# Earlier mask loads, no common start barrier, and the later attentions' head outputs moved from VectorE to ScalarE, in a four-layer kernel with a new written-out order

## What is computed

```python
scores = jnp.einsum('bhqd,bhkd->bhqk', q, k) / jnp.sqrt(jnp.float32(HD))
scores = scores * mask - 10000.0 * (1.0 - mask)      # layer 2
probs = jax.nn.softmax(scores, axis=-1)
return jnp.einsum('bhqk,bhkd->bhqd', probs, v)
```

## Time and profile before

| | |
|---|---|
| runs | 1038.15, 1041.89, 1042.33 us |
| profiled execution, its own time | 1040.13 us |
| its span (first to last instruction) | 1038.2 us |
| mean granted TensorE clock | 0.979 of full speed |
| busy: PE / weight loads | 954.2 / 760.8 us |
| busy: DVE / ACT / POOL | 745.7 / 587.8 / 540.6 us |
| HBM read and written | 26.85 and 2.10 MB |

### The profile page before, as it was taken

The page is one execution under the profiler, slowest core; times in us unless marked ns, Lnnn a source line. Parts: engine busy times, 40 slices in busy tenths (PEclk is TensorE's granted clock), DMA queues, the critical chain, the costliest instruction groups (busy, mean ns, idle before and its releaser), DMA issues.

```text
span 1038.2 us, 27531 instructions
## 1 busy us (share of the span) xinstructions
PE 954.2 (92%) x10944; PEld 760.8 (73%) x10944; DVE 745.7 (72%) x1607; ACT 587.8 (57%) x1334; POOL 540.6 (52%) x666
## 2 busy tenths in 40 slices
PE   6868999898799999999999999999998879999996
PEld 4657877676478787778778777777775758887885
DVE  1378358878889979844765578779589979876764
ACT  2379753235355556578867672546653347655772
POOL 1365355535568856433465474256565655765331
PEclk9979999999899999999999999999999989999999
DMA  9601200100000110100011100000010000000001
GB/s 351 248 3 33 55 1 1 29 1 1 1 1 3 33 33 1 55 22 1 20 34 29 33 2 25 5 22 3 2 29 13 2 2 2 13 2 14 13 2 42
DMA packets 27501, 30.70 MB, mean 30 GB/s; under 512 B 14640, under 2 KB 24176, under 8 KB 26736
## 3 DMA queue, kind: packets, MB, share of 16 engines
q1 hardware_dynamic: 26352, 27.11, 8.0%
q10 hardware_dynamic: 1024, 1.85, 0.5%
HBM read 26.85 MB, written 2.10 MB: 28 GB/s over the span
## 4 chain that ended last, share of the span: by engine, by line
PE 53%; DVE 20%; DVEq 9%; issue 6%; POOL 5%; ACT 4%; POOLq 1%; DMA 1%; ACTq 0%
PE bank L494 7%; PE bank L506 7%; PE bank L399 7%; PE bank L378 6%; PE bank L366 6%; PE bank L391 4%; DVE lane L1007 3%; DVEq L1010 3%; DVE bank L1003 2%; PE bank L457 2%; PE bank L481 2%; PE bank L535 2%; DVEq L1004 2%; PE bank L524 2%; DVEq L863 2%
## 5 line engine op out<-in xcount | busy, mean ns | idle before, releaser
L1413 POOL TENSOR_TENSOR lane<-lane 128x512 f32<-128x512 f32 x160 | 167.3, 1052 | 183.4 <-DVE lane L884 103.6
L1180 ACT COPY lane<-bank 128x512 f32<-128x512 f32 x232 | 132.2, 592 | 149.2 <-PE bank L366 83.7
L366 PE MATMUL bank<-ident,lane 128*128 128x128 f32 x896 | 133.3, 283 | 20.2 <-POOL lane L1413 4.8
L366 PEld LDWEIGHTS bank<-ident,lane 128*128 128x128 f32 x896 | 103.2, 144 | 49.3 <-issue 22.2
L1482 POOL TENSOR_TENSOR lane<-lane 128x512 f32<-128x512 f32 x64 | 81.3, 1271 | 74.1 <-DVE lane L1007 73.4
L1007 DVE TENSOR_TENSOR_SCAN lane<-lane,bank 128x256 f32<-128x256 f32 x128 | 81.0, 674 | 5.0 <-issue 0.4
L882 DVE TENSOR_REDUCE lane<-lane 128x8 f32<-128x512 f32 x96 | 64.8, 675 | 18.0 <-ACT lane L1199 16.8
L1162 ACT ACTIVATE lane<-bank,vecs 128x256 f32<-128x256 f32 x112 | 55.6, 554 | 39.0 <-PE bank L366 38.8
L1199 ACT ACTIVATE lane<-lane 128x512 f32<-128x512 f32 x96 | 60.7, 636 | 23.0 <-DVE lane L864 22.6
L1148 ACT ACTIVATE lane<-lane 128x256 f32<-128x256 f32 x96 | 52.4, 595 | 28.9 <-POOL lane L1398 28.7
L494 PE MATMUL bank<-lane,w_d 128*128 128x256 f32 x256 | 60.8, 387 | 2.6 <-ACT lane L1162 1.1
(11 more groups left out here) (162 smaller groups left out, 2233.3 us busy)
## 6 DMA issues: line engine op xcount, KB each, us to landing
lane<-in_inT SPq DMA_DIRECT2D x16, 256.0 KB, 4.6
lane<-in_x SPq DMA_DIRECT2D x16, 256.0 KB, 2.8
w_d<-in_w_d SPq DMA_DIRECT2D x1, 3072.0 KB, 21.2
w_am<-in_w_am SPq DMA_DIRECT2D x1, 2048.0 KB, 15.1
lane<-in_inT SPq DMA_DIRECT2D x16, 128.0 KB, 3.0
lane<-in_ctx SPq DMA_DIRECT2D x8, 256.0 KB, 2.9
out_x<-lane SPq DMA_DIRECT2D x8, 256.0 KB, 2.2
w_c<-in_w_c SPq DMA_DIRECT2D x1, 1792.0 KB, 12.0
```

The source lines that it names most:

```text
L366: ins = pe.transpose(t[:, i * P:(i + 1) * P], src, ident[:, :])
L1180: s.copy(out, src).then_inc(bk.free_sem(key), 1)
L1413: p.tensor_tensor(q, q, den.unsqueeze(2).to_broadcast([P, n, 512 // n]), ALU.mult).then_inc(sig["normal"].sem, 1)
```

## The change

1. `mask0` is loaded by one DMA that copies the row to all 128 partitions, without a wait for `ready`; POOL's memset of `mask0_raw` goes. SP's order has `w_am`, then the four masks, then `w_b`, `w_c`, `w_d` in a row.
2. `ready` is split. DVE, ACT wait only for DVE's small constants and POOL's memsets; the gate's tanh and `self_c` move into the first `s_b` and `v_b` of lane 0, with waits where they are used in the first round. POOL doesn't wait. PE waits for `vecs` and `ident` only before lane 0's (and each lane's) first transposition.
3. The heads of self-, cross- and layer-3 attention are taken by ACT (`s_heads`): the first pair after the copy of the third `probsT`, the second pair at the end. Layer 0's stay on DVE.
4. `ORDER` and `BANKS` are new throughout. DVE now has 737 steps, ACT 721.

```diff
-    ("in_loaded", 2, 16), ("mask0_loaded", 4, 16), ...
+    ("in_loaded", 2, 16), ("mask0_loaded", 1, 16), ...
 ORDER = {
     "PE": (
-        "P0111110000222223333031211010120011021221021101021011002203021012321130210111332111112330100000000001233130211"
...
+        "P0000022021112212133333001020201012122010110100120100112213120122000120120200000200211202101332021130311113312"
...
     "DVE": (
-        "P0110223030101100112222211001100221112211101100110002001220102221302230322330332331123233130033113013131000001"
...
+        "P0020001002212232230010011221120121001100010011001112110221012220312231322313222000300333311333330330102233112"
...
     "ACT": (
-        "P0111100022223333010122111001010220112211210101010012002210202312203321110233013321300103312033032113011110000"
...
+        "P0000220210112123233300001220112211001201001100110102112201212320213200012012221012021033033233331331000331320"
...
     "SP": (
-        "0123PP0123PP110022331023001122000011110222213323333301232013"
+        "0123P0123PPP002211330123002211330000111122202133332301230123"
...
-        ready = Signal("ready", 3)
+        ready = Signal("ready", 4)
...
             def probsT(u):
+                if g < NL and u == 0:
+                    pe.wait_ge(load["vecs"].sem, load["vecs"].at(0))
...
         def _(pe):
-            pe.wait_ge(load["vecs"].sem, load["vecs"].at(0))
...
                 if tag == "self":
+                    if g < NL:
+                        v.wait_ge(load["consts"].sem, load["consts"].at(0))
...
-            for c in range(2):
-                for i in range(2):
-                    v_heads(v, g, tag, c, i, A.headsT[:, c, i::2, :], VALUE_BIAS[tag])
-                yield
...
+            if g == 0:
+                v.wait_ge(load["consts"].sem, load["consts"].at(0))
+                v.tensor_scalar(self_c[:, :], self_m[:, :], 10000.0, -10000.0, ALU.mult, ALU.add).then_inc(ready.sem, 1)
...
         def _(v):
             v.wait_ge(load["vecs"].sem, load["vecs"].at(0))
-            v.wait_ge(load["consts"].sem, load["consts"].at(0))
...
-            v.wait_ge(ready.sem, ready.at(0))
+            v.wait_ge(ready.sem, ready.at(0, 2))
...
+        def s_heads(s, g, tag, A, c):
+
+            for h in range(2):
+                key = (g, tag, "heads", c, h)
+                s.wait_ge(bk.full_sem(key), bk.full_at(key))
+                src = bk.tile(key)[:, 0:2 * S].rearrange("p (b q) -> p b q", q=S)
+                bias = VALUE_BIAS[tag]
+                s.activation(A.headsT[:, c, h::2, :], src, ACT.Identity, bias=vec(bias, c) if bias else 0.0).then_inc(bk.free_sem(key), 1)
+
         def s_attention(s, g, tag, A):
...
+                if step == PT_:
+                    s_heads(s, g, tag, A, 0)
+                    yield
...
+            s_heads(s, g, tag, A, 1)
+            yield
...
+            if g == 0:
+                s.wait_ge(load["consts"].sem, load["consts"].at(0))
+                s.activation(tgate[:, 1:2], tgate[:, 0:1], ACT.Tanh).then_inc(ready.sem, 1)
...
-            s.wait_ge(load["consts"].sem, load["consts"].at(0))
-            s.activation(tgate[:, 1:2], tgate[:, 0:1], ACT.Tanh).then_inc(ready.sem, 1)
-            s.wait_ge(ready.sem, ready.at(0))
+            s.wait_ge(ready.sem, ready.at(0, 2))
...
         def p_a(p, g):
-            p.wait_ge(bk.full_sem((g, "l0", "q", 0)), bk.full_at((g, "l0", "q", 0)))
+            if g >= NL:
+                p.wait_ge(bk.full_sem((g, "l0", "q", 0)), bk.full_at((g, "l0", "q", 0)))
...
-            for lane_ in lanes:
-                p.memset(lane_.mask0_raw, 0)
             p.drain().then_inc(ready.sem, 1)
-            p.wait_ge(ready.sem, ready.at(0))
...
                 if g < NL:
                     sp_in(sp, g)
                     yield
-                    sp.wait_ge(ready.sem, ready.at(0))
...
-                for j in range(4):
-                    sp.dma_start(L.mask0_raw[32 * j:32 * j + 1, :], a["mask0"][g]).then_inc(sig["mask0_loaded"].sem, 16)
+                sp.dma_start(L.mask0_raw, a["mask0"][g].partition_broadcast(P)).then_inc(sig["mask0_loaded"].sem, 16)
```

More of the change, by code:

```diff
@@ new lines @@
+        "23222321000032133012303003021121100012122202302031101120222303333330001211332303000101213121000201203032102003"
+        "33203302022311033330202220002330131003131203020230202321223020303232101021301313103211132000122120312323330321"
+        "32131132212301231322220212211113111111211132113300031031000013200203231133311130301333211110000211200310333022"
+        "12003131131102021122102113013010103021321211111331111131223003333210000102221331011222012132102132103230003110"
+        "30320033200322320302220223223230101032133302303233123133013322120012032122202111300222301031121333230231030032"
@@ new lines @@
+        "30000001312200002213020101101012222201201112100213003210210000000012103212330220033230000000000203333300322122"
+        "30333012223212222322333112123211111132112210223222222123113323033333133113132111111031123310000300133133333203"
+        "33313100113213011010000110020212122200001000210023110011113111011012110211113313331313232222211223232100211223"
+        "21022122132233003321331210033211013330033300003303300032230310210110202110122331120312222220102332220011020030"
+        "30003002013332111101001113313011200200030000003303112310302313311213211111311222122232132222033233333133332022"
@@ L108 @@
-        "02033030302000313030323330330303213223322031321133133300300103030113012313333111131112112123020000120021113232"
-        "11332211332022231322111323212131233333221332222311132210200230322233332230032232230013233133223221313322003112"
-        "2030333113333"
+        "P0000220210112123233300001220112211001201001100110102112201212320213200012012221012021033233033331331000331320"
+        "23021131121222302312030330000001330000001200013010023032033220031003200222000011002002322102202202123231232132"
@@ new lines @@
+        "11131311213210322112210301023220332331333213211011311232322123100010013311111332133133000311031000121032230320"
+        "11113333111001002121102010022002103011212211310033121101122110213013300103321331211123332232123331122032210122"
+        "20121231321330332003002330332332232333203233323201022003213212001130101310103323003003000011001010111110202100"
+        "00100100312021000202033212313013132112332211102212233202331002233120332111313123232222303220200210013213120013"
+        "3332233222332031323233231323233320113221122131132213333223333"
@@ L117 @@
-        "323323223333300333301122212013333"
+        "P0213000212203012121010010112102203123122003003113303020230110000113220000221123210101222120101132120032200010"
+        "01030322030330000300223330031221303303002222223312121121131213222221213312333311332112113123120300133111330333"
+        "30033331100110021120020210111110120123133132211223300121211212310301321030120013030003030002231311012023223112"
+        "02022221213322200030300330013311010110233110020300001330310100022331111131232122212233233313123212312223222323"
@@ L118 @@
+        "200033232333233203333112212133233"
     ),
     "SP": (
-        "0123PP0123PP110022331023001122000011110222213323333301232013"
+        "0123P0123PPP002211330123002211330000111122202133332301230123"
     ),
@@ L123 @@
 BANKS = (
[L124 to L133, removed]
+    "01234567012345670156720156726720672063742741201756562436503641051735710603064253064257235721305721305273015273"
+    "01523651204516702467520745207631452076315240152764370654274207657462513704625174307564163451062475124741547152"
+    "03202043271450361402735614730256147306214730562014627513634621727253467102505025052341026317250356372154637632"
+    "67321657312644042650427504327150643042304760237146054602504623237235713575137042651370261431740532174063521062"
+    "35610235461023546102361025367431604371607431024375103725140737532713524726407104326735672310540754602754306271"
+    "53406271563042715304271427574251732540173254016712673152675263475261043170453104210574631740263401567532427635"
+    "46203754176235167243014623462734061234506210261034726510347367235417026351635177027026473047230547631266126361"
+    "36205620542051473262056140404703570605716403572160435276104352437542367157054702547023754602160232607236723564"
+    "17203564107235641064712067342540640275346012701205327324057364126570314657203143026154370216543617524306751274"
+    "253170542316705416"
 )
@@ L1120, in v_d @@
             v.wait_ge(bk.full_sem(key), bk.full_at(key))
+            if g < NL:
+                v.wait_ge(ready.sem, ready.at(0))
             v.scalar_tensor_tensor(flat(x[:, :, :]), bk.tile(key)[:, :], tgate[:, 1:2], flat(x[:, :, :]), ALU.mult, ALU.add).then_inc(bk.free_sem(key), 1)
@@ L1422, in p_attention @@
                     if tag == "self":
+                        if g < NL:
+                            p.wait_ge(ready.sem, ready.at(0))
                         q = grid(A.probs[step])
```

27 lines of the change are left out of this document (4 added, 23 removed).

## The result

The changed kernel takes 1052.36 us (median of 4, 1045.27 to 1057.89), the kernel before 1041.16 us in the same series. The ratio is 1.0116 [1.008, 1.0152]: slower by 1.2%, where 1.1% faster was forecast, and above the range of 1013 to 1047. The four times follow the granted clock: 1045.27 us at a mean of 0.980, 1057.89 at 0.967.

The account below looks back on a forecast made before the run. PE was taken to bound the kernel, busy 954.2 of 1038.2 us. The terms -1.2 - 6.3 - 6 + 2 + 1 gave -10.5 us on 1040.13, so 1030 us was predicted, range 1013 to 1047.

Parts of the forecast that it names:

- What bounds the kernel: Whole kernel: PE bounds it, busy 954.2 of 1038.2 us; the change is worth what it does to 84 idle us.
- the prediction's last sentence: Forecast is wrong if PE's busy sum is unchanged and its idle time from 130 to 1010 us exceeds 51 us.
- Start of PE: Kernel start: PE begins at 6.8 us instead of 8.32, and 2.4 us of waiting for loads is dropped.
- the masks: Before lane 0's first scores: PE stalls 3.0 us on the mask; start and masks together gain 1.2 us.
- Scores among the projections: From 43 to 90 us: four units of exponentials done earlier take 6.3 us off PE's 16.1 us of idle time.
- Heads: Attention heads moved from DVE to ACT: 6 us gained in DVE-dense stretches, 2 and 1 us charged back.
- The new strings: New engine orders, with each round's 32 scan steps contiguous on DVE: charged 0, bounds -8 (gain) to +16 us.
- Rival B: Where four lanes scan together, scans crowd DVE and PE idles more: slower, 1046 to 1062 us; chance 0.15.
- Rival A: The start's gain is given back later, waiting for DVE in scan stretches: no change, 1037 to 1041 us; chance 0.2.
- Rival C: At the start the mask holds PE, stall 7.5 us or no gain there: still faster, 1034 or 1037; chance 0.15.

Follow-up runs that it names:

- old_order_both_edits: All edits of the change (early masks, split barrier, later heads on ScalarE) under the orders of the kernel before: 1034.49 us, ratio 0.9964.

## Why the prediction was wrong

*What bounds the kernel* was right, and the prediction's last sentence named the case that came: PE's idle time from 130 to 1010 rose to 60.4 us, over the 51 set as the mark, with PE's busy sum up by 0.6% only.

*Start of PE, the masks* had the right times, in part by luck. The first matmul came at 6.96 for 6.8, the mask at 20.0 for 20.5, the scores at 21.91 inside 21 to 22. But the stall of 3.0 us in front of them wasn't there: PE could have begun them at 21.8 at the earliest, not at 18.9. Its first seven steps took 14.9 us instead of 12.0, because the matmuls of the first `q` and `k0` started at half pace until 12.5 us. The 2.4 us that I read as waiting for loads in the kernel before, and dropped, were the same thing: there too the first matmuls stand 427 ns apart, without a gap. Two errors of 3 us cancelled.

*Scores among the projections* held under the new order. 43 to 90 gained 6.1 of the 6.3 us, and PE's idle time to 130 us fell by 7.5, as much as both terms together. The clock that PE kept there, another 3.7 us, wasn't in the sum. Taking the early masks and barriers away again cost 7 us. Under the old order a like move, with lanes 0 and 1, gave nothing.

*Heads* was right in mechanism. I took 3 net; the old order gave 1.7, the new one 15, within the bounds but five times the term. DVE's total came to 719 for 715, ACT's to 593 for 604, with 45 table loads for 48.

*The new strings* is the step that failed: "I charge 0, bounds -8 (gain) to +16". With the same edits the new strings cost 16 us, where the edits together are worth 4 in the old order. The 16 are even net of the early scores, which the forecast counts as a term of its own though they are part of the strings. By the two traces the strings give back some 10 us before 130 and lose 24.2 behind it, in idle time (11.9) and in clock (12.3), which the sum has nowhere. So the term that I set to nothing because it couldn't be read was the largest of all, and by itself it lies beyond its bound of 16.

The sum then reads: edits under the old order -0.36%, strings +1.53%, together +1.16%. The edits rescue part of what the order loses: without the heads on ScalarE the new strings cost 1.0262 / 0.9992, 28 us; with them 16. That is why edits that are worth 7 and 15 us under the new order don't add up to a gain over the kernel before.

*Rival B* had the sign and the place (stretches dense with scans), not the mechanism. It decides, I wrote, once PE idles over 10.5 us more there: the dense stretches idle 39.2 for 36.4, and with 44 us of scan work gone the distance stayed at 1.0116. What differs from 240 to 270 us is what PE has beside the scans. *Rival A* is right in that the start was given back later, but not for lack of DVE time. *Rival C* didn't come.

Shown: the order costs the 16 us; banks, ScalarE's load and the mask don't, nor does DVE's throughput account for most of it. Shown too is that orders shifted by some ten places lose 6%, whichever way. Not shown is whether the phase of the lanes has a share. That the new strings lose by the same mechanism, steps placed ahead of their data, fits their pattern (idle engines, clock lost behind PE's gaps, DVE's waits at L815 twice those of the old order), but no run undid it step by step. Which of their places cost is open.

## What to carry to other kernels

Where a change brings a new written-out order for in-order engines, the order is a term of its own, and here it was the largest: charge it with what the order may lose, not with zero, and don't price the edits as if the old interleaving stayed. Run the edits under the old order first; here that alone gave the kernel that beats both, 1034.49 us. Judge an order by the work that TensorE has beside the serial stretches: here a gap there was paid again in clock. An order fitted to one kernel's timing can lose several per cent when lanes are shifted by hand, as both of these did.

## What the runs showed that I had not expected

- Shifting two lanes by at most 12 us, no step over 11 places, costs 6.4 to 6.6% in either direction, while changing 868 of 1008 entries of the bank string leaves the ratio at 1.0 [0.999, 1.0009].
- Of the order's 17.4 us, 8.9 are TensorE's clock: PE fell to 1.2 GHz for 14 us at 248 to 262 after PE had worked for only 3.9 of the 8 us before, among the scan chains. In the kernel before that happened at 50 to 64 us, behind the idle time before the first softmax, and the change did remove that one.
- PE's first matmuls of `q` start 427 ns apart and not 216, in both kernels. The slow pace ends near 12.5 us in both traces, so of the 1.4 us by which PE started earlier only about half was gained (in old_order_both_edits it ends at 10.0 us).
- The same edit, 96 heads copies moved from DVE to ScalarE, is worth 0.16% or 1.4%, depending on the order around it.
